# Leaving out the two small VectorE passes per batch that negate the LayerNorm means

## The reference

```
mod = (silu(c) @ wmod).reshape(32, 6, 1, 128)        # sa, ca, ga, sb, cb, gb
ga, gb = (2*(g >= 0) - 1) * max(|g|, 0.25)
h = layernorm(x) * (1 + ca) + sa                     # (x - mean) / sqrt(var + 1e-5)
q, k, v = h @ W + b, reshaped raw to (b, 16 heads, 8, 256)
attn = softmax(einsum('bhdt,bhds->bhts', k, v) * temperature)
x = x + ga * einsum('bhdt,bhts->bhds', q, attn)
h = layernorm(x) * (1 + cb) + sb
x = x + gb * ffn(h)       # gate and up 128 -> 352, silu(gate)*up, down; every operand
                          # quantised to FP4 in blocks of 16 with a scale of max|.|/6
```

## Time and profile before

| what | value |
|---|---|
| median of the runs | 612.01 us (610.42 to 612.53) |
| span of the profiled execution | 611.3 us |
| PE busy | 558.3 us (91%), 4336 matmuls |
| DVE busy | 568.7 us (93%), 1124 instructions |
| ACT busy | 555.9 us (91%), 2281 instructions |
| POOL busy | 507.3 us (83%), 710 instructions |
| DVE var, line 1013 | 64 instructions, 9.6 us busy, 150 ns each |
| DVE nm, line 1016 | 64 instructions, 9.3 us busy, 145 ns each |

### The profile page before, as it was taken

The page is one execution under the profiler, slowest core; times in us unless marked ns, Lnnn a source line. Parts: engine busy times, 40 slices in busy tenths (PEclk is TensorE's granted clock), DMA queues, the critical chain, the costliest instruction groups (busy, mean ns, idle before and its releaser), DMA issues.

```text
span 611.3 us, 15522 instructions
## 1 busy us (share of the span) xinstructions
PE 558.3 (91%) x4336; PEld 385.6 (63%) x4336; DVE 568.7 (93%) x1124; ACT 555.9 (91%) x2281; POOL 507.3 (83%) x710
## 2 busy tenths in 40 slices
PE   4588999999999999999999999999999999998874
PEld 2465556666666666666666666666666666666653
DVE  5568799999999999999999999999999999999986
ACT  2499899999999999999999999999999999999621
POOL 5544478999999999999999999999999999988741
PEclk9669899999999999999999999999999999999878
DMA  5655556546655556555655556655655556652000
GB/s 156 179 142 143 129 152 163 145 133 170 170 140 147 149 155 173 159 157 137 172 144 143 149 155 171 171 145 139 170 144 141 152 153 174 164 143 58 10 10 26
DMA packets 87888, 86.12 MB, mean 141 GB/s; under 512 B 8566, under 2 KB 83548, under 8 KB 87804
## 3 DMA queue, kind: packets, MB, share of 16 engines
q1 hardware_dynamic: 85372, 83.10, 50.4%
q10 hardware_dynamic: 2432, 2.03, 1.2%
HBM read 47.29 MB, written 37.81 MB: 139 GB/s over the span
## 4 chain that ended last, share of the span: by engine, by line
ACT 52%; PE 18%; issue 13%; DVE 12%; POOL 3%; ACTq 1%; DVEq 0%; POOLq 0%
ACT probs L825 47%; DVE neg_max L1005 6%; PE score_ps L1502 6%; PE bank L1581 5%; PE bank L1570 3%; ACT hT L835 2%; DVE silu_g L1123 2%; ACT hid_T L859 2%; PE bank L1548 2%; PE bank L1606 1%; ACT q_T L841 1%; DVE h_mag L975 1%; POOL hid_q L367 1%; PE bank L1520 1%; DVE h_mag L979 1%
## 5 line engine op out<-in xcount | busy, mean ns | idle before, releaser
L825 ACT ACTIVATE probs<-score_ps,neg_max 128x256 f32<-128x256 f32 x1024 | 483.5, 552 | 5.4 <-DVE neg_max L1005 4.3
L1005 DVE TENSOR_REDUCE neg_max<-score_ps 128x4 f32<-128x1024 f32 x256 | 312.1, 1219 | 19.5 <-PE score_ps L1502 16.8
L825 ACT ACTIVATION_READ_ACCUMULATOR probs<-score_ps,neg_max 128x1 f32 x1024 | 292.4, 286 | 0.0
L1502 PE MATMUL score_ps<-v_stack,k_stack 128*128 128x256 f32 x1024 | 234.9, 333 | 24.2 <-ACT probs L825 21.7
L1502 PEld LDWEIGHTS score_ps<-v_stack,k_stack 128*128 128x128 f32 x1024 | 156.0, 194 | 108.2 <-ACT probs L825 85.1
L1548 PE MATMUL bank<-probs,q_z 128*32 128x256 f32 x2048 | 132.6, 389 | 0.0
L1548 PEld LDWEIGHTS bank<-probs,q_z 128*32 128x32 f32 x2048 | 57.6, 111 | 42.4 <-issue 3.2
L1606 PEld LDWEIGHTS bank<-wd_T,hid_T 118*128 118x128 f32 x384 | 52.7, 201 | 7.6 <-ACT hid_T L859 1.3
L1606 PE MATMUL bank<-wd_T,hid_T 118*128 118x128 f32 x384 | 56.0, 286 | 0.5 <-ACT hid_T L859 0.5
L1570 PE MATMUL bank<-wgu_T,h_T 128*128 128x352 f32 x128 | 52.0, 488 | 1.7 <-ACT h_T L848 0.5
L367 POOL TENSOR_TENSOR hid_q<-hid_r,hid_sc 128x704 f32<-128x704 bf16 x31 | 43.0, 1387 | 7.6 <-DVE hid_r L362 7.5
(11 more groups left out here) (119 smaller groups left out, 880.9 us busy)
## 6 DMA issues: line engine op xcount, KB each, us to landing
split_dram<-kv_hi SPq DMA_DIRECT2D x124, 128.0 KB, 2.6
split_dram<-kv_lo SPq DMA_DIRECT2D x124, 128.0 KB, 2.6
k_stack<-split_dram SPq DMA_DIRECT2D x124, 128.0 KB, 4.5
v_stack<-split_dram SPq DMA_DIRECT2D x31, 512.0 KB, 4.2
mod_bc<-mod_dram SPq DMA_DIRECT2D x32, 256.0 KB, 4.0
x_in<-in_L_attn_x_dram SPq DMA_DIRECT2D x32, 128.0 KB, 3.1
out_dram<-out_t SPq DMA_DIRECT2D x32, 128.0 KB, 3.6
split_dram<-kv_hi ACTq DMA_DIRECT2D x4, 128.0 KB, 2.4
```

What stands on the lines that cost most here:

```text
L825: nc.scalar.activation(probs[p][:, h, a, :], score_ps[:, j % 4, a, :], ACT.Exp, bias=neg_max[:, p, n:n + 1], accum_out=row_sum[:, p, h, a: ...
L1005: nc.vector.tensor_reduce(neg_max[:, p, 4 * u:4 * u + 4], score_ps[:, lo:lo + 2, :, :].rearrange("p b a n -> p (b a) n"), AX.X, ALU.max, n ...
L1502: done = nc.tensor.matmul(score_ps[:, j % 4, a, :], k_stack[p][:, h, 128 * a:128 * a + 128], v_stack[p][:, h // R, :], start=True, stop=True)
```

## The change

The 64 calls of minus_mean go, and with them the tiles nm1 and nm2 and their semaphores. Whoever added minus the mean now subtracts the mean, read as a one-column operand straight out of stats (mean_of). The normalising instructions of GpSimd wait for rstd alone; bn_stats now waits for the normalising instruction of the batch two before, since that one reads the half of stats that it overwrites. TensorE's gates matmul has a semaphore of its own, and two more waits in front of it, on things that an earlier matmul has waited for already. No order is changed.

```diff
+        def mean_of(stats, c, a):
+            return stats[:, c % 2, 1 + 3 * a:2 + 3 * a]
 ...
         def normalise2_on(eng, ve, b, c):
             wait_batches(eng, rstd2_made, b + 1)
-            wait_batches(eng, nm2_made, b + 1)
             wait_batches(eng, h2_made, b)
             for a in range(2):
-                ve.tensor_scalar(h2_c[:, a, :], x1[:, c, a, :],
-                                        nm2[:, a:a + 1], rstd2[:, a:a + 1],
-                                        ALU.add, ALU.mult).then_inc(h2_c_made, 1)
+                ve.tensor_scalar(h2_c[:, a, :], x1[:, c, a, :], mean_of(stats2, c, a), rstd2[:, a:a + 1],
+                                 ALU.subtract, ALU.mult).then_inc(h2_c_made, 1)
 ...
             def normalise1(b, c):
                 wait_batches(pool, rstd1_made, b + 1)
-                wait_batches(pool, nm1_made, b + 1)
                 wait_batches(pool, xT_made, b)
                 for a in range(2):
-                    nc.gpsimd.tensor_scalar(xn[:, a, :], x_in[:, b % NX, a, :],
-                                            nm1[:, a:a + 1], rstd1[:, a:a + 1],
-                                            ALU.add, ALU.mult).then_inc(xn_made, 1)
+                    nc.gpsimd.tensor_scalar(xn[:, a, :], x_in[:, b % NX, a, :], mean_of(stats1, c, a),
+                                            rstd1[:, a:a + 1], ALU.subtract, ALU.mult).then_inc(xn_made, 1)
 ...
             def gates():          # VectorE
-                dve.wait_ge(pre_pe, 3)
+                dve.wait_ge(gates_ps_made, 1)
 ...
-            def minus_mean(nm, stats, p):
-                return nc.vector.tensor_reduce(nm[:, :], stats[:, p, 1:6:3].unsqueeze(2), AX.X, ALU.max, negate=True)
 ...
             def stats1_rows(b, c):
                 wait_in(dve, x_loaded, b)
-                wait_batches(dve, nm1_made, b - 1)
+                wait_batches(dve, xn_made, b - 1, 2)
 ...
             def variance1(b, c):
                 ...
                 variance(var1, stats1, c % 2).then_inc(var1_made, 1)
-                wait_batches(dve, xn_made, b, 2)
-                minus_mean(nm1, stats1, c % 2).then_inc(nm1_made, 1)
 ...
             def stats2_rows(b, c):
                 wait_batches(dve, x1_made, b + 1)
-                wait_batches(dve, nm2_made, b - 1)
+                wait_batches(dve, h2_c_made, b - 1, 2)
 ...
             def variance2(b, c):
                 ...
                 variance(var2, stats2, c % 2).then_inc(var2_made, 1)
-                wait_batches(dve, h2_c_made, b, 2)
-                minus_mean(nm2, stats2, c % 2).then_inc(nm2_made, 1)
 ...
             def scaled_norm2(b, c):          # VectorE, the last batch alone
-                dve.wait_ge(nm2_made, b + 1)
+                dve.wait_ge(stats2_made, b + 1)
 ...
-                        out=h2_c[:, a, :], in0=x1[:, c, a, :], scalar=nm2[:, a:a + 1], in1=mod_bc[:, b % NX, 2, :],
-                        op0=ALU.add, op1=ALU.mult).then_inc(h2_c_made, 1)
+                        out=h2_c[:, a, :], in0=x1[:, c, a, :], scalar=mean_of(stats2, c, a), in1=mod_bc[:, b % NX, 2, :],
+                        op0=ALU.subtract, op1=ALU.mult).then_inc(h2_c_made, 1)
 ...
             def gates():          # TensorE
+                pe.wait_ge(silu_c_made, 1)
+                pe.wait_ge(wmod_in, 16)
                 nc.tensor.matmul(score_ps[0:NB, 3, :, :].rearrange("b a n -> b (a n)"), silu_c[:, :],
-                                 w_mod[:, 2 * D:6 * D], start=True, stop=True).then_inc(pre_pe, 1)
+                                 w_mod[:, 2 * D:6 * D], start=True, stop=True).then_inc(gates_ps_made, 1)
```

More of the change, by code:

```diff
@@ L80, in adaln_block @@
         var1, var2 = sb("var1", [128, 2]), sb("var2", [128, 2])
-        nm1, nm2 = sb("nm1", [128, 2]), sb("nm2", [128, 2])
         rstd1, rstd2 = sb("rstd1", [128, 2]), sb("rstd2", [128, 2])
@@ L125, in adaln_block @@
         k_zeroed = [sem(f"k_zeroed{i}") for i in range(2)]
-        pre_pe, pre_act, silu_c_made, modT_made, mod_step, mod_stored, bias_step = (
-            sem(n) for n in ("pre_pe", "pre_act", "silu_c_made", "modT_made", "mod_step", "mod_stored", "bias_step"))
+        pre_pe, pre_act, silu_c_made, modT_made, gates_ps_made, mod_step, mod_stored, bias_step = (
+            sem(n) for n in ("pre_pe", "pre_act", "silu_c_made", "modT_made", "gates_ps_made", "mod_step",
+                             "mod_stored", "bias_step"))
         x_loaded = [sem(f"x_loaded{i}") for i in range(NX)]
@@ L135, in adaln_block @@
         eps_made = sem("eps_made")
-        stats1_made, var1_made, nm1_made, rstd1_made, stats2_made, var2_made, nm2_made, rstd2_made = (
-            sem(n) for n in ("stats1_made", "var1_made", "nm1_made", "rstd1_made", "stats2_made", "var2_made",
-                             "nm2_made", "rstd2_made"))
+        stats1_made, var1_made, rstd1_made, stats2_made, var2_made, rstd2_made = (
+            sem(n) for n in ("stats1_made", "var1_made", "rstd1_made", "stats2_made", "var2_made", "rstd2_made"))
         xn_made, xT_made, hT_made = sem("xn_made"), sem("xT_made"), sem("hT_made")
```

## The result

| | before | after |
|---|---|---|
| median of the runs | 612.27 us (4 runs: the three named at the start and one of 612.86) | 647.41 us (4 runs: 645.04, 646.84, 647.98 and one of 1227.8) |
| span of the profiled execution | 611.3 us | 645.1 us |
| granted TensorE clock, mean | 0.962 | 0.971 |

The ratio is 1.057, 95% interval [1.053, 1.061]; the single execution of 1227.8 us is not in it, and without it the median of the changed kernel is 646.84 us. The forecast was 611.9 us, the range 610.0 to 613.0.

A forecast was written before the change was run, and what follows sets the result against it. The prediction took ScalarE, waiting once a batch for a maximum held back by TensorE's scores, to bound the kernel. Steps 0, start 0, tail -0.06 gave a 611.2 us span, plus 0.7 for the median: 611.9 us, range 610.0 to 613.0.

The forecast's parts named there:

- The passes nm1 and nm2: VectorE's negated-mean passes of the first and second norm, in the steps: removing 0.06 us of queue each gains 0.
- the cover: Work hiding the removed passes: TensorE's scores end the first norm's wait; ScalarE, 0.16 us behind, hides the second's.
- Rival A: VectorE's time comes back in the steps: 610.3 us, or 608.2 if all 64 passes return 0.06 us; chance 0.07.
- Its smaller form: Only the piece of nm on the chain of waits returns, 1.7 us: 610.3 us.
- Waits and gates: Changed waits of GpSimd, bn_stats and TensorE's gates matmul: taken as 0, at most 0.28 us once for gates.
- The operand: GpSimd's normalising passes read a stats column and subtract: taken as 0, bounded by 0.87 us a batch.
- Rival C: Slower: GpSimd's new operand is dearer, in xn ahead of TensorE's transposes; 0.2 us more per pass gives 617 us; chance 0.05.
- reserve of 0.22 us: Slack between TensorE's hidden-layer transposes ending at 310.89 and ScalarE taking them at 311.11, before dearer xn passes reach ScalarE.
- The tail: After the steps, at the last second norm, VectorE's queue is partly the path: removing nm gives -0.06 us.
- rival B: The tail is dealt anew: h_c gets ahead of GpSimd's pass, up to -1.4 us, 610.5 us; chance 0.13.
- the encounter: In the tail, the second h_c on VectorE waits for GpSimd's 1.39 us pass; both move by 0.06 us, so it stays.

The follow-up runs named there:

- kernel 3: The changed kernel with add instead of subtract in GpSimd's normalising instructions (wrong sign of the mean): 612.33 us, ratio 0.9985 to the kernel before.
- kernel 4: The kernel before with each of its two negating passes made twice, the first time into an unread tile: 610.70 us, ratio 0.9986.
- run 1: The changed kernel with four forms of GpSimd's normalising instruction: add or subtract, each with a column of stats or of a constant tile: 627.6 us.
- kernel C: The changed kernel with GpSimd's subtract alone, (subtract, mult) by two written numbers, add alone, and tensor_tensor subtract in the four normalising passes: 624.5 us.
- Run 6: The changed kernel with half of GpSimd's pass h_c times scale left out: 637.97 us, ratio 1.043 to the kernel before.
- 5: The changed kernel with subtract only in the first norm (626.56 us), only in the second (626.70), or only in the second xn pass (616.69); add elsewhere.
- 2: The kernel before with its nm passes kept but not negated, and subtract instead of add in GpSimd's normalising instructions: 647.14 us, ratio 1.054.

## Why the prediction was wrong

*The passes nm1 and nm2: right.* I took 0 for both, with TensorE's scores and ScalarE's own queue as the cover. Runs 3 and 4 show it from both sides, and the maximum that starts 0.03 us behind the scores shows the reason. Rival A (VectorE's time comes back, 610.3 or 608.2) is refuted: twice the passes should have cost 3.8 us, and cost nothing that can be measured. Its smaller form, 1.7 us, lies within the interval of kernel 3 but not of kernel 4, and it wanted a shorter batch, where kernel 3 has 17.21 us against 17.18. One remark was off: I expected VectorE's busy time to fall by some 9 us. It fell by 2.1 in kernel 3 (568.7 to 566.6), since most of a pass of 0.145 us lay under its neighbours.

*Waits and gates: right in sum.* Kernel 3 has them all. At the gates matmul, the answer to the earlier trace rows, VectorE shows 0.58 us idle in the changed kernel and none in kernel 3, against 0.28; the two have the same code there, and the start as a whole differs from run to run by up to 2 us (the first exponential at 24.7 in kernel 3, at 26.7 in the changed kernel), so that is scatter, not the change.

*The operand: this step failed.* It read: "0 at one end, as much again (0.87 us a batch) at the other. I take 0: it is one value per partition for 128 elements, and the nearest row is the same instruction with the same number of operands." Two things were wrong. The nearest row was not the same instruction: its operations were (add, mult), and run 1 shows that these, not the operand, carry the price. And I bounded the xn pair alone; h_c has two more such passes. The term, taken as 0, is 4 x 0.35 - 0.19 = 1.21 us a batch, over 28 batches 34 us, where the span grew by 33.8. That the two agree so closely is in part luck: between the first and the last exponential it grew by 32.4, ahead of them by 2.1 (the scatter just named), behind them it fell by 0.8. The trace of before even held a tensor_scalar with another pair, (mult, max), on GpSimd, its operands two numbers written into the instruction:

```profile
L283 POOL TENSOR_SCALAR hid_sc<-hid_am 128x44 f32<-128x44 f32 x28 | 10.4, 371 | 1.9 <-DVE hid_am L970 1.9
L283 POOL TENSOR_SCALAR h_sc<-h_am 128x16 f32<-128x16 f32 x30 | 8.4, 280 | 3.6 <-DVE h_am L970 1.1
```

28 elements more cost 91 ns, 3.25 ns each. Carried on to 128 elements that is 371 + 84 x 3.25 = 644 ns, clearly above the 448 of (add, mult) at the same width. This row would have said: another operation has another price, up to 0.2 us a pass or more. That is 0.8 a batch less the reserve, 17 us or more, a forecast of about 629. It would still have been too low: 644 ns is what kernel C then showed for a pair with two numbers (0.65), and with columns the pair takes 0.80.

*Rival C: the right event, wrong in cause and place.* I gave "GpSimd's new operand is dearer" 0.05 and wrote that nothing in the trace pointed to a price. The event is what happened: GpSimd's passes became dearer, by 0.35 us and not the 0.2 of my example. Its reserve of 0.22 us a batch is near the measured 0.19 by luck, not for the reason given. I read it from TensorE's transposes of the hidden layer and ScalarE. Run 6 shows that the reserve is that of GpSimd's queue against ScalarE's period: 0.28 us taken out between h_c and h come back in full.

Why does GpSimd bind at 94% busy (17.38 of 18.43)? The busy times don't tell: ScalarE's is a little higher in that batch (17.44). The chain in order of time goes through its queue and in the batch from 300 us on leaves it for VectorE only here:

```profile
300.95 0.64 POOL h_q L334
...
301.61 0.04 DVE h_mag L974
...
301.82 0.16 DVE var L1012
...
302.05 0.71 POOL rstd L550
```

GpSimd makes h_q, VectorE's h_mag waits for it with var queued behind, and GpSimd's next instruction, rstd, waits for var: 0.47 us of idle that belong to the ring. Whether var ahead of h_mag would free them was not tried.

*The tail (rival B): dealt anew, and worth little.* I took -0.06 with the encounter unchanged, because "Both GpSimd's pass and the h_c passes start from hid_rs". That was wrong as well. The rows that answer to the earlier trace rows:

```profile
616.16 0.52 DVE L1243 SCALAR_TENSOR_TENSOR h_c<-x,stats,mod_bc 128x128 f32<-128x128 f32 x2
616.43 1.49 POOL L341 TENSOR_TENSOR hid_q<-hid,hid_rs 128x704 f32<-128x704 f32 x1
616.72 1.62 DVE L1252 SCALAR_TENSOR_TENSOR h<-h_c,rstd,mod_bc 128x128 f32<-128x128 f32 x2
```

Both h_c passes now get through (0.52 us in place of 1.70), and the first h is held instead (the pair 1.62 in place of 0.61). The rows just ahead show why, before and then in the changed kernel:

```profile
581.24 0.70 POOL L563 TENSOR_TENSOR rstd<-var,minus_half 128x2 f32<-128x2 f32 x1 [0.16 <-DVE var L1013]
```

```profile
615.60 0.19 DVE L286 TENSOR_SCALAR hid_sc<-hid_am 128x44 f32<-128x44 f32 x1
615.76 0.71 POOL L562 TENSOR_TENSOR rstd<-var,minus_half 128x2 f32<-128x2 f32 x1 [0.16 <-DVE var L1012]
615.82 0.43 DVE L1134 RECIPROCAL hid_rs<-hid_sc 128x44 f32<-128x44 f32 x1
```

Before, GpSimd was through with rstd at 581.94, and its pass at 582.07 came 0.08 us after the end of hid_rs. Now the idle 0.24 ahead of hid_rs is gone together with nm, hid_rs ends at 616.25, and GpSimd is still in rstd then; its pass follows straight on that, at 616.43, 0.27 us after the first h_c and not 0.17, and the second h_c starts 0.10 ahead of it. In kernel 4 the idle is gone too, but nm stands there twice, and the second h_c still starts 0.01 behind GpSimd. Why the idle goes, no run shows.

From the last exponential's end to the end of h it is 6.82 us before and 6.52 in kernel 3: 0.3 us won, not 1.4. All kernels with nm have 6.68 to 6.82, the changed kernel and those of 3, 5 and 6 have 6.39 to 6.52. The kernels that keep nm (2 and 4) still have a second h_c of 1.52 us; those without it have the held h. By the rule of the Trainium skill's "SBUF — State Buffer", section "Who interferes with whom", as the prediction cites it, h is held up by the same GpSimd pass, so that an earlier h_c brings little. The trace agrees: the first h takes 1.36 us, the second 0.34. Note also that VectorE's own h_c takes 0.25 us with subtract as with add, so the price is GpSimd's alone.

The Trainium skill's "GPSIMD Engine Reference", section "3.1 Elementwise — side-by-side cycle accounting", puts the 2.6 cycles an element of tensor_tensor down to its two inputs, and gives no price by operation. By it alone the two pairs would cost the same; here they take 0.45 and 0.80 us, and the measurement decides.

## What to carry to other kernels

An instruction's price is known only for the operations that the trace shows: when a change swaps add for subtract, the row of add is a neighbour and not the price, and every instruction with the new operation is to be counted. An engine at 93% (15.96 of 17.18 us) beside a full one can be a second bound at close range: compute how much it can take (here 0.19 us a batch) before work on it is made dearer, and take the sum of its queue, not one place. Removing 0.06 us passes from an engine that is busy but not waited for brought nothing that could be measured (ratio 0.9985 [0.9967, 1.0003]).

## What was unexpected in the hardware

- GpSimd's tensor_scalar at 128x128 in f32: 0.45 us for (add, mult) and (mult, mult), 0.80 for the seven other pairs tried with columns as operands ((subtract, mult), (max, mult), (add, add), (add, subtract), (add, max), (subtract, subtract), (max, max)), 0.62 for a single subtract, 0.65 for (subtract, mult) with two numbers in the instruction. tensor_tensor with a repeated column: 0.39. In VectorE's scalar_tensor_tensor add and subtract take the same.
- A queue 94% busy can be the bound, beside one that is busy for as long (17.38 and 17.44 of 18.43 us): period = 15.04 us + the four passes, over eight kernels to 0.03 us, with one 0.1 us off.
